# Causal attention and top-2 experts in one kernel: part of a head group's value product moves from step 7 to step 5

## The reference

```python
# attention, 16 heads of 32, on the layer-normed x
qp = q @ Wq.T
k, v = jnp.split(latent_kv @ Wkv_expand.T, 2, axis=-1)
scores = jnp.einsum('bhqd,bhkd->bhqk', qh, kh) * inv_sqrt_d
scores = jnp.where(causal, scores, jnp.finfo(scores.dtype).min)
out = jnp.einsum('bhqk,bhkd->bhqd', softmax(scores), vh)
x = x + out @ Wout.T
# experts, on the layer-normed x: a top-2 choice per token and output from 8 router outputs
logits = (h @ router_w.T + router_b).reshape(T, O, E)
w, sel = jax.lax.top_k(probs, 2)          # then divided by their sum
c = zeros((T, E)).at[t_idx, sel].add(w)
x = x + jnp.einsum('te,teo->to', c, jnp.einsum('th,eoh->teo', h, expert_w) + expert_b)
```

## Time and profile before

| | us |
|---|---|
| median of 3 runs (lowest, highest) | 1996.52 (1996.43, 1997.9) |
| the profiled execution | 1994.92 |
| its span, first to last instruction | 1993.2 |
| PE busy in the span | 1910.6 |
| VectorE, ScalarE, GpSimd busy | 1435.2, 1037.8, 867.2 |

### The profile page before, as it was taken

How to read it: one execution, slowest core, us unless ns; L and a number is a source line. 1 busy time by engine, 2 the same in 40 slices (tenths; PEclk the granted TensorE clock), 3 DMA queues, 4 the chain that set the end, 5 groups by cost and what they waited for, 6 DMA issues and landing times.

```text
span 1993.2 us, 30400 instructions
## 1 busy us (share of the span) xinstructions
PE 1910.6 (96%) x9756; PEld 1512.5 (76%) x9756; DVE 1435.2 (72%) x2840; ACT 1037.8 (52%) x2062; POOL 867.2 (44%) x1024
## 2 busy tenths in 40 slices
PE   4899999999996999999999999899999999999999
PEld 3666776767763788888888888688888888888887
DVE  5667667767668658787888888477777777777732
ACT  2566566566554347877777787433344333344400
POOL 5577777777677235455444435101221111132100
PEclk8999999999997999999999999899999999999999
DMA  5454555455465477786756555822232222223110
GB/s 165 119 126 129 136 143 129 126 144 138 104 177 192 165 242 259 230 280 222 253 207 216 186 188 196 322 73 79 79 124 93 79 86 93 79 83 124 52 42 32
DMA packets 103549, 294.54 MB, mean 148 GB/s; under 512 B 13761, under 2 KB 14785, under 8 KB 98338
## 3 DMA queue, kind: packets, MB, share of 16 engines
q1 hardware_dynamic: 91394, 210.23, 32.9%
q10 hardware_dynamic: 8736, 66.59, 10.4%
q0 software_dynamic: 3328, 16.78, 3.6%
HBM read 150.31 MB, written 109.16 MB: 130 GB/s over the span
## 4 chain that ended last, share of the span: by engine, by line
PE 87%; DVE 5%; ACT 2%; DMA 2%; issue 2%; POOL 2%; SPq 0%; ACTq 0%; DVEq 0%; POOLq 0%
PE pair L260 21%; PE pair L262 21%; PE pair L261 21%; PE pair L670 4%; PE ps L716 3%; PE pair L703 3%; PE ps L260 3%; PE ps L261 3%; PE ps L262 3%; DVE pair L1374 1%; PE ps L736 1%; ACT pT L1090 1%; PE ps L897 1%; DVE nmax L1368 1%; DMA lg_all<-ev_a 1%
## 5 line engine op out<-in xcount | busy, mean ns | idle before, releaser
L260 PE MATMUL pair<-w_h,hT 128*128 128x512 f32 x1920 | 751.2, 391 | 8.3 <-DVE w_l L1676 8.3
L262 PE MATMUL pair<-w_h,hT 128*128 128x512 f32 x1920 | 748.0, 390 | 0.0
L261 PE MATMUL pair<-w_l,hT 128*128 128x512 f32 x1920 | 748.0, 390 | 0.0
L1885 POOL TENSOR_TENSOR logits<-logits,second 128x512 f32<-128x512 f32 x224 | 298.4, 1370 | 596.7 <-DVE second L1584 596.4
L260 PEld LDWEIGHTS pair<-w_h,hT 128*128 128x128 f32 x1920 | 360.9, 188 | 82.9 <-issue 8.7
L262 PEld LDWEIGHTS pair<-w_h,hT 128*128 128x128 f32 x1920 | 360.8, 188 | 75.8
L261 PEld LDWEIGHTS pair<-w_l,hT 128*128 128x128 f32 x1920 | 361.1, 188 | 74.2
L1687 DVE SCALAR_TENSOR_TENSOR xb<-pair,c_all,xb 128x512 f32<-128x512 f32 x256 | 191.8, 749 | 198.2 <-PE pair L262 191.9
L1090 ACT ACTIVATE pT<-pair,zero 128x1024 f32<-128x1024 f32 (+3 forms) x256 | 202.5, 792 | 197.1 <-PE pair L703 194.2
L1374 DVE CUSTOM_DVE_ANT_0 pair<-pair,future 128x256 f32<-128x256 f32 (+3 forms) x340 | 184.2, 554 | 124.1 <-PE pair L670 115.6
L1184 ACT ACTIVATE w<-tree 128x512 f32<-128x512 f32 x32 | 20.3, 634 | 390.7 <-DVE tree L1586 390.7
(11 more groups left out here) (163 smaller groups left out, 2618.6 us busy)
## 6 DMA issues: line engine op xcount, KB each, us to landing
logits<-lg_all ACTq DMA_DIRECT2D x32, 1792.0 KB, 8.7
qk_st<-qk SPq DMA_DIRECT2D x372, 128.0 KB, 2.4
lg_all<-ev_a SPq DMA_DIRECT2D x33, 768.0 KB, 8.3
lg_all<-ev_b SPq DMA_DIRECT2D x31, 768.0 KB, 3.3
xb<-x SPq DMA_DIRECT2D x64, 256.0 KB, 3.0
hT_all<-hT SPq DMA_DIRECT2D x32, 512.0 KB, 4.2
hT<-hT_all SPq DMA_DIRECT2D x32, 512.0 KB, 4.1
xt<-in_x SPq DMA_DIRECT2D x8, 1024.0 KB, 5.4
```

The source lines that it names most:

```text
L260: pe.matmul(dst, lh, rh, start=start, stop=False)
L261: pe.matmul(dst, lh, rl, start=False, stop=False)
L262: return pe.matmul(dst, ll, rh, start=False, stop=stop)
L1885: pool.tensor_tensor(logits[t % 2][:, e - 1, :], logits[t % 2][:, e - 1, :], second[:], ALU.subtract)\
```

## The change

On PE, groups 0 to 2 do the first sums and values of key blocks 0 and 1 in step 5, at its end, with the turned maxima between the sums and the values; group 3 keeps them in step 7. `r_ps` moves to other columns of the same bank. The output projection's pieces get a table of steps of their own (`OUT_AT`), VectorE's residual sums another (`SUMMED_AT`). The keys made in group 3 move to step 6 and to the other `j_ps` bank. SyncE copies the shift rows ahead of the residual loads, and stores the last sum after the stacking. Batch 1 is written out ahead of the loop. In the last batch three router weights in place of four are prepared before the epilogue, outputs are split at earlier steps, and two low parts are made later. In the last router block ScalarE has a buffer (`ev_d`) for logits 3 and 4 and issues the first store itself; the other stores go between the expert loads. Left out below: semaphore names, `wo_read`'s signal, the same `SPLIT_LAST` on GpSimd, and the helper `project_query`, which holds the three lines that it replaces.

```diff
 ev_c = ffn("ev_c", [P, O], F32)
+ev_d = ffn("ev_d", [P, 2, O], F32)
 junk = ffn("junk", [P, O], BF16)
 ...
 d_ps = ps[1]
-r_ps = d_ps[0:HC * QB, 0:P]
+r_ps = d_ps[0:HC * QB, P:2 * P]
 last_o_ps, last_d_ps = j_ps
 ...
 SPLIT = {(3, 5): 0, (3, 6): 1, (0, 1): -2, (0, 6): -1}
+SPLIT_LAST = {(3, 0): 0, (3, 2): 1, (0, 1): -2, (0, 6): -1}
 ADDS = 2 * (QB - 1)
 ...
-    return 1 if c in (1, 2) else 0
+    return 1 if c else 0
 ...
-    return 6 if c in (1, 2) else 5
-
-OUT_FIRST = ((1, 0), (1, 6), (2, 3), (3, 0))
+    return 6 if c else 5
+
+OUT_AT = (((1, 0), (1, 1), (1, 2), (1, 3)), ((1, 6), (1, 7), (2, 0), (2, 1)),
+          ((2, 2), (2, 3), (2, 5), (2, 7)), ((3, 2), (3, 4), (3, 5), (3, 6)))
+SUMMED_AT = ((1, 4), (2, 2), (3, 0), (3, 7))
 OUT_FIRST_LAST = ((1, 0), (1, 4), (2, 0), (2, 4))
 ...
-    return {0: (0, 5), 1: (1, 7), 2: (2, 7), 3: (3, 6)}[c]
+    return (c, 7 if c else 5)
 ...
 EXPERT_FIXES = 2 * NE
-FIXED = ((0, 6), (0, 7), (2, 0), (2, 1), (2, 7), (3, 0))
+FIXED = ((0, 6), (0, 7), (2, 0), (2, 7), (3, 0), (3, 1))
 FIXES = 5
-FIX_EARLY = {(2, 5): ((0, 0),), (2, 6): ((0, 1), (0, 2)), (2, 7): ((0, 3), (0, 4)),
-             (3, 0): ((1, 0), (1, 1)), (3, 1): ((1, 2), (1, 3), (1, 4)), (3, 3): ((2, 0), (2, 1)),
-             (3, 4): ((2, 2), (2, 3), (2, 4)), (3, 6): ((3, 0), (3, 1)), (3, 7): ((3, 2), (3, 3), (3, 4))}
-HI_EARLY = ((3, 1), (3, 3), (3, 6))
-LO_EARLY = ((3, 2), (3, 5))
+FIX_EARLY = {(2, 5): ((0, 0), (0, 1)), (2, 6): ((0, 2), (0, 3), (0, 4)), (2, 7): ((1, 0), (1, 1)),
+             (3, 0): ((1, 2), (1, 3), (1, 4)), (3, 1): ((2, 0), (2, 1)), (3, 2): ((2, 2), (2, 3), (2, 4))}
+HI_EARLY = ((3, 1), (3, 4), (3, 6))
+LO_EARLY = ((3, 3),)
 ...
-    for i, (c0, v0) in enumerate(OUT_FIRST_LAST if last else OUT_FIRST):
+    if not last:
+        for i, steps in enumerate(OUT_AT):
+            if (c, v) in steps:
+                return i, steps.index((c, v))
+        return None
+    for i, (c0, v0) in enumerate(OUT_FIRST_LAST):
         chunk = (c - c0) * UNITS + v - v0
 ...
     body(0, True, True, True)
-    with eng.Fori(1, B - 2) as b:
+    body(1, False, True, True)
+    with eng.Fori(2, B - 2) as b:
         body(b, False, True, True)
 ...
                     store_sum(b - 1, 0)
-                    load_residual(b - 1, 2)
                 elif c == 2:
                     store_sum(b - 1, 1)
-                    load_residual(b - 1, 3)
                 else:
                     store_sum(b - 1, 2)
-                    store_sum(b - 1, 3)
             if more or c < KC - 1:
                 rows(n + 1, (c + 1) % KC)
+            if not first and c in (1, 2):
+                load_residual(b - 1, c + 1)
             if more or c == 0:
                 stack(n + AHEAD, (c + AHEAD) % KC)
+            if not first and c == KC - 1:
+                store_sum(b - 1, KC - 1)
             if c == 0 and further:
 ...
         load_expert(e)
-        if e == 2:
-            store_logits(t, "a", 3, ev_a[:], 0, 3)
+        if e == 4:
+            store_logits(t, "b", 5, ev_d[:], 3, 5)
+        if e == 5:
+            store_logits(t, "c", 6, ev_c[:].rearrange("p (e o) -> p e o", o=O), 5, 6)
+    store_logits(t, "c", 7, ev_a[:, 0:1, :], 6, 7)
     load_turned(1, 1)
-    store_logits(t, "b", 6, ev_a[:], 3, 6)
-    store_logits(t, "c", 7, ev_c[:].rearrange("p (e o) -> p e o", o=O), 6, 7)
 ...
                            tile_position=(0, hh * HD), skip_group_check=True)
-        if kb > 0:
-            mm.then_inc(s["pv"], 1)
+        mm.then_inc(s["pv"], 1)
 ...
+        pe.wait_ge(s["causal"], n * UNITS + 2)
+        if some(n):
+            pe.wait_ge(s["refined"], 2 * n)
         if turned:
 ...
         for hh in range(HC):
-            mm = pe.matmul(d_ps[hh * HD:(hh + 1) * HD, 0:P], ones[:], pT[0][:, hh, 0:P],
-                           start=True, stop=True, tile_position=(0, hh * HD), skip_group_check=True)
-        mm.then_inc(s["pv"], 1)
+            pe.matmul(d_ps[hh * HD:(hh + 1) * HD, 0:P], ones[:], pT[0][:, hh, 0:P],
+                      start=True, stop=True, tile_position=(0, hh * HD), skip_group_check=True)
 ...
         last = not more
-        held = [("K", b * KC + AHEAD - 1), ("Q", b * KC + AHEAD - 1)]
+        held = [("K", AHEAD - 1), ("Q", AHEAD - 1)] if first else \
+            [("WO", (b - 1) * QB - 1), ("K", b * KC + AHEAD - 1)]
 ...
                     values(VALUE[v])
-                if v in QUERY and ahead:
-                    if QUERY[v] == 0:
-                        take(1, "Q", n + AHEAD)
-                    queries(n + AHEAD, (c + AHEAD) % KC, QUERY[v])
+                if v in QUERY and ahead and (c, v) != (1, 0):
+                    project_query(v)
                 if v == SUMMED and not (first and c == 0):
 ...
                     keys((c + AHEAD) % KC, b if c == 0 else b + 1, key_bank(c))
-                if v == LAST and not final:
+                if v == LAST and c == KC - 1 and not final:
+                    first_sums(n, True)
                     values_of(n, c, b, 0)
-                    first_sums(n, more or c < KC - 1)
                     values_of(n, c, b, 1)
 ...
                         scores(n + g, (c + g) % KC, vv, (0,))
+                if (c, v) == (1, 0) and ahead:
+                    project_query(v)
+                if v == TURN and c < KC - 1:
+                    first_sums(n, False)
                 if v == TURN and (more or c < KC - 1):
                     turn_maxima(n + 1, c + 1)
+                if v == TURN and c < KC - 1:
+                    values_of(n, c, b, 0)
+                    values_of(n, c, b, 1)
 ...
         act.wait_ge(s["o_ok"], n + 1)
-        if c == 0 and some(b * QB):
-            act.wait_ge(s["wo_mm"], b * QB)
+        if c < 2 and some(b):
+            act.wait_ge(s["wo_read"], (b - 1) * 2 + c + 1)
         act.activation(oT_h[:, c, :], o_sb[OUT_BUF[c]][:], ACT.Copy).then_inc(s["o_hi"], 1)
 ...
                     hi_shift(n + 1)
-                if (c, v) in SPLIT and not (first and c == 0):
-                    d = SPLIT[c, v]
+                split = SPLIT_LAST if last else SPLIT
+                if (c, v) in split and not (first and c == 0):
+                    d = split[c, v]
                     if first:
 ...
         if e == ND:
-            act.wait_ge(s["lg_out_b"], NT * 16)
+            act.wait_ge(s["lg_out_c"], (NT + 1) * 16)
         act.activation(w_h[:, e], w_raw[:, e], ACT.Copy).then_inc(s["ew_hi"], 1)
 ...
         act.wait_ge(s["lg_mm"], t * ND + k + 1)
-        if t == NT - 1 and k == 3:
-            act.wait_ge(s["lg_out_a"], NT * 16)
-        elif k in (0, 3, 6):
-            act.wait_ge(s[f"lg_out_{'abc'[k // 3]}"], t * 16)
-        dst = ev_c[:] if k == 6 else (ev_a, ev_a if t == NT - 1 else ev_b)[k // 3][:, k % 3, :]
+        if t < NT - 1:
+            if k in (0, 3, 6):
+                act.wait_ge(s[f"lg_out_{'abc'[k // 3]}"], t * 16)
+            dst = ev_c[:] if k == 6 else (ev_a, ev_b)[k // 3][:, k % 3, :]
+        else:
+            if k in (0, 5):
+                act.wait_ge(s["lg_out_a" if k == 0 else "lg_out_c"], t * 16)
+            if k == 6:
+                act.wait_ge(s["lg_out_a"], NT * 16)
+            dst = (ev_a[:, 0, :], ev_a[:, 1, :], ev_a[:, 2, :], ev_d[:, 0, :], ev_d[:, 1, :], ev_c[:],
+                   ev_a[:, 0, :])[k]
         act.activation(dst, l_ps[k % 4], ACT.Copy).then_inc(s["lg_ok"], 1)
+        if t == NT - 1 and k == 2:
+            act.wait_ge(s["lg_ok"], t * ND + 3)
+            act.dma_start(logits_of(t, 0, 3), ev_a[:]).then_inc(s["lg_out_a"], 16)
 ...
         mean_variance(1, 1, "ln2")
-        lo_router(2)
         norm2(0, 0)
         norm2(1, 1)
+        lo_router(1)
         lo_block(0, 0)
 ...
         lo_block(1, 1)
+        lo_router(2)
 ...
                 fix_router(k, q)
+        whole(3)
         whole(4)
```

More of the change, by code:

```diff
@@ L206, in build @@
             k_mm k_hi k_lo stacked0 stacked1 st_ones v_mm v_ok scores negmax turned nm_hi nm_lo rows_in shifted exps causal added pv summed
-            logs recips refined o_ok o_hi o_lo wo_mm x1_ok xr_in0 xr_in1 x1_out0 x1_out1
+            logs recips refined o_ok o_hi o_lo wo_mm wo_read x1_ok xr_in0 xr_in1 x1_out0 x1_out1
             fw_hi fw_lo prep_in prep_ok prep_out base_in late_in fw_fix fixed fix_erows one_ok xb_in ln2_st ln2_var ln2_rs ln2_nm ln2_nb hn_ok
@@ L326, in summed_block @@
         def summed_block(c, v, last):
-            step = c * UNITS + v - (0 if last else 1)
-            at = out_block(step // UNITS, step % UNITS, last)
+            if not last:
+                return SUMMED_AT.index((c, v)) if (c, v) in SUMMED_AT else None
+            at = out_block(c, v, last)
             return at[0] if at and at[1] == KC - 1 else None
@@ L612, in freed @@
                              "LNT": ("xT_hi", "xT_lo"), "WO": ("x1_ok",)}[task]:
-                    pe.wait_ge(s[name], k + 1)
+                    if some(k + 1):
+                        pe.wait_ge(s[name], k + 1)
             def norm_turn(g, i, bank):
```

(13 more changed lines are left out.)

## The result

The changed kernel takes **2022.07 us** (median of 4 runs, 2021.02 to 2023.26) beside 1996.47 for the kernel before: ratio **1.0122, 95% interval 1.0111 to 1.0134**. The direction was forecast, the size was not: 25.6 us where 12.2 were expected, outside the range. The span of the profiled execution is 2019.6 us, 26.4 above the one before.

| stage | before | after | change | forecast |
|---|---|---|---|---|
| ahead of batch 0 | 54.51 | 55.09 | +0.6 | 0 |
| batch 0 | 67.69 | 74.59 | +6.9 | +4.85 |
| batches 1 to 6 | 435.69 | 453.43 | +17.7 | +14.3 |
| batch 7, groups 0 to 2 | 57.46 | 63.11 | +5.65 | +1.55 |
| group 3 to the first router matmul | 41.04 | 34.68 | −6.4 | −6 |

A forecast was written before the change was run, and what follows sets the result against it. TensorE, busy 96% of the span, was taken as the bound. Terms 12.8 + 4.1 + 1.3 + 6.0 − 3.0 − 0.5 − 1.5 − 7.0 = +12.2 us on 1994.92, plus 1.6 to the median, gave 2008.7 us; range 1997 to 2015.

The forecast's parts named there:

- Part 1: Groups 0 to 2: moved values uncover the shift rows' 4.2 us path; +12.8 batches 1 to 6, +4.1 batch 0, +1.3 batch 7.
- Part 2: Step 5: turned maxima between narrow matmuls change the array's form twice more; 0.25 us for each of 24 groups, +6.0.
- Part 3: Output blocks spread over other steps cover waits for maxima: −0.5 us a batch, −3.0 over six; batch 7, group 0, −0.5.
- Part 4: End of attention: −6 for PE's GpSimd wait, +4.5 for the fourth weight in the router's chain; net −1.5 us.
- Part 5: Router to experts: logits copy with its own buffer no longer waits for a store; −7.0 us, bounds −5 and −10.
- the two entries: Measured form changes around a transpose beside narrow matmuls: 0.14 us in and about 0.11 out, taken as 0.25 a group.
- the rivals: No new change of form, 0.15; shorter rows' path, 0.15; attention's end gives its whole 11 us, 0.12; worse wait, 0.1.
- The wait is worse: Last rival: at the last group PE stands 6 us or more, clock falls to 1.2 GHz; 2014 us, chance 0.1.

The follow-up runs named there:

- the first run: The changed kernel with the first sums and values 0 and 1 back in step 7 in groups 0 to 2: 1989.88 us, 0.9965.
- the two repaired kernels: Changed kernel, nm_l between the heads' maxima, turned maxima behind the narrow matmuls: output blocks at old steps 2015.61 us, at the change's steps 2008.33 us.
- the kernel with the waits filled: Changed kernel with idle PE matmuls ahead of the shift-row waits of groups 2 and 3, batches 0 to 6: 2015.14 us (2012.60 to 2022.03), 1.0086.
- the third run: The changed kernel with VectorE making nm_l between the two heads' maxima in groups 1 and 2: 2010.37 us, 1.0068.

## Why the prediction was wrong

- **Part 1, the rows' path: the mechanism right, the steady size nearly so.** +0.7 and +1.4 in a steady batch were forecast; the gaps of PE there are 0.91 and 1.59 us, 0.74 and 1.42 beyond the last score's streaming. Group 1 gave back 0.65 in its step 0, which the sum lacked. In batch 0 the part was sized too high: +6.9 were measured, 3.7 of them clock, so 3.2 against 4.85; group 2 there had already taken 1.1 us longer in step 5 before the change. Batch 7 was sized too low: PE waits for rows 9.9 us in four pieces, where it waited 4.7 in two. Group 1's rows, which were called early, landed 5.0 us after their issue (3.5 before the change), beside weight and stacking DMAs, in place of the 1.8 us median that the sum took.
- **Part 2, the changes of form: right.** 0.25 a group forecast, 0.3 measured.
- **Part 3, the output blocks: the sign depends on the rest.** −0.5 a batch was forecast. With the values back in step 7 the spreading costs 0.3 (output blocks at their old steps, against the first run); with the move in place it saves, 2.2 between the two repaired kernels. In the changed kernel itself it was not taken out alone, but batches of 74.98 beside 75.31 speak for a gain near the forecast. It is no part of the miss.
- **Part 4, the end of attention: right in sum.** −6 forecast for PE's wait and −6.4 found; of the two edits named for it, the earlier `oT_l` alone gives nothing. The router lost 6.35 instead of 4.5: one wait of 3.1 us for ScalarE, followed by 1.6 us of slow clock.
- **Part 5, router to experts:** −7 forecast, −4.45 measured. ScalarE no longer waits for the store but for the first weight, whose conversion starts at 1313.61, and PE waits 4.1 us, where under 3 were forecast:

```profile
1313.61 1.91 ACT L1222 ACTIVATE w_h<-w_raw 128x2048 fp32r<-128x2048 f32 x1 [7.14 <-DMA w_raw<-w_fix]
```

- **The step that failed: the sum prices a wait of PE at its own length.** The clock behind it is a term put at nothing without a reason, and it measured 9.5 us, 7.9 of them behind waits for the rows and 1.6 in the router. The prediction had the two halves in its hands, show the clock at 0.56 behind the idle stretch before the experts, and the last rival even names it for the last group. It was not applied to the waits of 1.5 to 2 us that the change itself creates. The miss between the spans is 26.4 − 12.2 = 14.2. By stage it is 9.5 of clock, 2.55 of part 5, 2.5 more in groups 0 to 2 of batch 7, and −0.4 for all else, where batch 0 (−1.65) and batches 1 to 6 (+0.8) partly cancel. The clock alone takes the forecast from 2008.7 to 2018.2, out of its range.
- Of the rivals, none happened. *The wait is worse* was the nearest: its mechanism is what came, at six places and not at one.

## What to carry to other kernels

When work is moved earlier on the engine that bounds, look at what it now stands in front of, and what it used to cover: here 1.86 us of matmuls were both the cover of a 4.2 us path through VectorE, SyncE and a DMA, and after the move a delay at its head. Price new waits of TensorE like these (1.6 to 3.1 us) with the clock behind them too, here 1.0 to 2.6 us more where it fell, and treat it as uncertain whether it falls. And undo the parts one by one: the rest of this change was worth 7 us (0.35%) which the move hid, and all kernels without the move ran faster than the kernel before. But the worth of one part holds for the company that it was measured in: the output blocks' new steps cost 0.3 us a batch without the move and save 2.2 in the repaired kernel with it.

## What was not expected of the hardware

- **The length of one wait does not decide the clock.** In batch 4 PE stood for 1.59 us with 0.33 us of matmuls in it and kept its clock (the windows above). In batch 5 the like wait

```profile
488.74:490.34 1.60, 0.33 (x2) 0.06 (x1) 1.54 (x5) 0.49 (x1) 0.99 (x2) 1.00 0.04 10
...
492.43:494.42 1.99, 1.99 (x11) 1.05 (x15) 1.89 (x9) 0.82 (x1) 1.31 (x4) 0.56 0.89 205
```

  was followed by 1.2 GHz, 2.1 us after its end. Four runs of the kernel with the waits filled scatter over 9.4 us, four of the changed kernel over 2.2, and the kernel before over 7.3 in all its runs. Whether it is the clock that differs between runs isn't shown, with one profile for each kernel.
- **A GpSimd select of 0.41 us took 10.61 while VectorE ran operations with two SBUF operands nearly back to back** (the third run). The next GpSimd instruction starts at 638.52, so the engine was held for that long. It isn't always so one-sided: in the changed kernel, from 636.21 on, two such VectorE operations took 3.57 us where the third run has 2.34, and a select beside them took 1.39. The Trainium skill (GPSIMD Engine Reference, Key points) says that the engine shares its SBUF interfaces with VectorE and contends with "DVE instructions in a 2-port perf mode or with two SBUF inputs". The trace agrees, with 10.61 us for a work of 0.41; no run here took the pieces away at that place.
- **A transpose between narrow matmuls costs 0.3 us a time,** more than the two entries' 0.14 and 0.11 on which the 0.25 rested.
